# A depthwise convolution in front of an expert layer: normalising by channels, a ring of spread bands, and the next block's front inside the convolution

## What is computed

```python
def _L0_conv_ref(x, w_large, w_small, ...):      # depthwise: one 13x13 and one 3x3 kernel for each channel
    large = bn(dwconv(x, w_large, 6), g_l, b_l, m_l, v_l)
    small = bn(dwconv(x, w_small, 1), g_s, b_s, m_s, v_s)
    return large + small + bn(x, g_i, b_i, m_i, v_i)
...
x = x + _L0_conv_ref(_ln_c(x), ...)              # _ln_c: mean and variance over the 96 channels of a pixel
t = _to_tokens(x)
t = t + _L0_ffn_ref(_ln_t(t), ...)               # 4 experts 96 -> 384 -> 96, the two best by a softmax gate
```

## Time and profile before

| | |
|---|---|
| median of 3 runs | 1277.17 us (1275.31 to 1277.45) |
| the profiled execution: time, and span of its profile | 1275.62 us, 1273.5 us |
| busy over the span: PE, PEld, DVE, ACT, POOL | 92%, 80%, 63%, 38%, 20% |
| mean granted TensorE clock | 0.957 of full speed |
| TensorE's first instruction; first convolution matmul; end of the last one; first `moe_up` matmul | 25.4, 30.1, 86.5, 98.6 us |

### The profile page before, as it was taken

One profiled execution on the slowest core, in us unless ns is written; L12 is line 12 of the kernel. 1 busy time (PEld: TensorE's weight loads), 2 busy tenths in 40 slices (PEclk: granted clock), 3 DMA queues, 4 the chain that ended last, 5 costly groups with the idle time before them and its releaser, 6 DMA issues. The chain is left out here.

```text
span 1273.5 us, 24179 instructions
## 1 busy us (share of the span) xinstructions
PE 1171.1 (92%) x8528; PEld 1024.4 (80%) x8528; DVE 807.9 (63%) x2916; ACT 482.4 (38%) x944; POOL 254.0 (20%) x234
## 2 busy tenths in 40 slices
PE   1979999947999999999999999999999998999776
PEld 1978999946999999899997767767999987887555
DVE  6036676646666665587775565655777767776646
ACT  3514334323555544334431323223334322332442
POOL 3002112122010100312122333332221222211200
PEclk9998999977999999899999999999999999999786
DMA  3301000010000000000000000000000000000000
GB/s 136 86 4 66 20 31 19 1 50 1 2 2 1 2 1 1 2 1 0 0 1 1 2 1 2 2 1 2 1 1 0 0 1 1 1 1 4 1 11 37
DMA packets 11562, 15.69 MB, mean 12 GB/s; under 512 B 7385, under 2 KB 9007, under 8 KB 11346
## 3 DMA queue, kind: packets, MB, share of 16 engines
q1 hardware_dynamic: 10754, 12.86, 3.1%
q10 hardware_dynamic: 720, 1.66, 0.3%
HBM read 11.37 MB, written 3.15 MB: 11 GB/s over the span
## 5 line engine op out<-in xcount | busy, mean ns | idle before, releaser
L955 PEld LDWEIGHTS moe_dn<-all_w,moe_hid 128*128 128x128 f32 x2304 | 269.9, 192 | 5.4
L955 PE MATMUL moe_dn<-all_w,moe_hid 128*128 128x96 f32 x2304 | 271.7, 275 | 0.0
L890 ACT ACTIVATE moe_hid<-moe_up 128x512 f32<-128x512 f32 x288 | 169.7, 598 | 231.2 <-PE moe_up L947 218.1
L945 PE MATMUL moe_up<-front_xh,front_w1h 97*128 97x512 f32 x288 | 121.9, 423 | 0.6 <-PEq L1005 0.3
L835 DVE SCALAR_TENSOR_TENSOR all_X<-moe_dn,front_gate,all_X 128x96 f32 (+1 forms) x384 | 95.3, 310 | 30.5 <-PE moe_dn L955 24.4
L947 PE MATMUL moe_up<-front_xl,front_w1h 97*128 97x512 f32 x288 | 113.8, 395 | 0.0
L946 PE MATMUL moe_up<-front_xh,front_w1l 97*128 97x512 f32 x288 | 113.3, 393 | 0.0
L827 DVE SCALAR_TENSOR_TENSOR all_X<-all_b,front_gate,all_X 128x96 f32 (+1 forms) x384 | 100.8, 324 | 6.2 <-DVE front_var L81 2.8
L786 POOL TENSOR_TENSOR front_prob<-front_euler,front_logit 128x16 f32<-128x16 f32 x21 | 60.9, 2901 | 189.9 <-DVEq L414 189.9
L1386 PE MATMUL l1c_o<-l1c_vs,l1c_pt 128*128 128x64 f32 x768 | 94.4, 277 | 0.5 <-DVE l1c_ro L1164 0.5
L1386 PEld LDWEIGHTS l1c_o<-l1c_vs,l1c_pt 128*128 128x128 f32 x768 | 91.8, 195 | 2.9 <-issue 0.9
(11 more groups left out here) (401 smaller groups left out, 2019.5 us busy)
## 6 DMA issues: line engine op xcount, KB each, us to landing
all_w<-w SPq DMA_DIRECT2D x3, 582.0 KB
all_w<-w SPq DMA_DIRECT2D x3, 576.0 KB
all_X<-x_rows SPq DMA_DIRECT2D x2, 768.0 KB, 6.8
conv_scratch<-all_X SPq DMA_DIRECT2D x2, 768.0 KB, 3.2
all_X<-conv_scratch SPq DMA_DIRECT2D x2, 768.0 KB, 4.7
out_tokens<-l3f_y SPq DMA_DIRECT2D x5, 288.0 KB, 2.1
l0c_band<-band ACTq DMA_DIRECT2D x1, 1248.0 KB, 9.3
all_b<-b SPq DMA_DIRECT2D x3, 192.0 KB
```

The source lines that it names most:

```text
L890: act.activation(hid[:, n, :], up[n % UPS][:, :], ACT.Gelu).then_inc(hid_done, 1)
L945: pe.matmul(bank, w1h[:, n, :], xh[:, p, :], start=True, stop=False)
L955: last = pe.matmul(dn[e % 2][:, j * C:(j + 1) * C], hid[:, n, j * P:(j + 1) * P], w2[:, n, :], start=(k == 0), stop=(k == KC - 1))
```

## The change

In `l0_conv`:
- The tokens are normalised by channels in three chunks (channels 0 to 15, 16 to 47, 48 to 95). For each chunk and half of the images there are two instructions, a subtraction that reads `X` with the tile as the inner dimension, and a product in place. Turn 0 needs chunk 0 alone; turns 1 to 5 are moved behind convolution pieces 0, 1, 2, 4 and 6.
- POOL's power for the batch norms is cut in two: 9 values for groups 0 to 2 first, then the tokens' two powers, then 27 values.
- `full` is a ring of six groups, filled group by group, three groups ahead.
- Groups 10 and 11 are done by halves of the images, first half first: pieces (10, half 0), (11, half 0), (10, half 1), (11, half 1), so 14 pieces in all.
- The expert layer's front is moved into this block: its weights are split behind pieces 4 to 9, its constants are set early, and its statistics, normalising and transposes follow the adding back of piece 11, which completes the first half of the images. The first convolution's `dve_binarise` is cut in two around it.

In `moe`, layer 0 keeps of the front only the gate's matmuls, logits, softmax and choice; the choice comes behind the statistics of step 1.

```diff
@@ WeightWork
-    def dve_binarise(self, dve, chain):
+    def dve_differences(self, dve, chain):
         dve.wait_ge(self.signs, 1)
         dve.tensor_tensor(sg[0:C, 0, :], sg[0:C, 0, :], w1[0:C, :], ALU.subtract)
         chain.sync(dve.tensor_tensor(sg[:, 1, 0:KC * C], sg[:, 1, 0:KC * C], w2f, ALU.subtract))
+    def dve_binarise(self, dve, chain):
         dve.tensor_tensor(w1[0:C, :], w1[0:C, :], sg[0:C, 0, :], ALU.add)
         dve.tensor_tensor(w2f, w2f, sg[:, 1, 0:KC * C], ALU.add)
@@ l0_conv
+        RF, FIRST = 6, 3
+        CHUNKS = (0, 2 * GC, 6 * GC, C)
-        full = s.sb("full", [P, NG * KL, GC, SIDE])
+        full = s.sb("full", [P, RF, KL, GC, SIDE])
+        F = T["front"].begin(s, T, 0, front_tp, None)
+        SPLIT = NG - 2
+        PIECES = [(g, 0, 2) for g in range(SPLIT)] + [(g, h, h + 1) for h in range(2) for g in range(SPLIT, NG)]
+        TURN_AFTER = {0: 1, 1: 2, 2: 3, 4: 4, 6: 5}
@@ gpsimd
-            pool.tensor_tensor(inv[:, :, :], shift[:, :, :], mhalf[:, :].rearrange("p (k g) -> p k g", k=3),
-                               ALU.pow).then_inc(bn_pow, 1)
+            factors(0, FIRST)
...
+            factors(FIRST, NG)
+            F.pool_consts(pool)
+            F.pool_rstd(pool)
@@ scalar
+            def fill(g):
+                act.wait_ge(band_done, 1 if g < FIRST else 2)
+                if g >= RF:
+                    act.wait_ge(conv_done, g - RF + 1)
                 for k in range(GC):
+                    last = act.activation(full[:, g % RF, :, k, :], band[:, g, :, :], ACT.Copy, scale=own[:, k:k + 1])
...
+            fill(0)
+            tokens_out(0)
+            fill(1)
+            fill(2)
+            for n in range(NP):
+                if n in TURN_AFTER:
+                    tokens_out(TURN_AFTER[n])
+                conv_copy(n)
+                if n + 3 < NG:
+                    fill(n + 3)
+                if 4 <= n < 4 + NE:
+                    F.act_weights(act, n - 4)
+                if n == 8:
+                    F.act_consts(act)
+                if n == SPLIT + 1:
+                    work.act_signs(act)
+            F.act_tokens(act)
@@ vector
+            def normalise(c):
+                lo, hi = CHUNKS[c], CHUNKS[c + 1]
+                for h, half in enumerate(halves):
...
+                    out = xn[:, h, lo:hi, :]
+                    chain.sync(dve.tensor_tensor(out, x0[:, half, lo:hi].rearrange("p t c -> p c t"), wide(mean),
+                                                 ALU.subtract))
+                    last = dve.tensor_tensor(out, out, wide(rstd), ALU.mult)
+                last.then_inc(xn_done, 1)
+            merge_bands(0, 0, FIRST)
+            for c in range(len(CHUNKS) - 1):
+                normalise(c)
+            merge_bands(1, FIRST, NG)
...
+            for n in range(NP):
+                add_back(n)
+                if n == NG - 6:
                     work.dve_sums(dve, chain)
+                if 6 <= n < 6 + NE:
+                    F.dve_weights(dve, n - 6)
+                if n == NG - 3:
                     work.dve_centre(dve, chain)
+                if n == SPLIT + 1:
+                    dve.wait_ge(back_out, n + 1)
+                    F.dve_stats(dve, chain)
+                    work.dve_differences(dve, chain)
+                    F.dve_apply(dve, chain)
+                if n == SPLIT + 2:
+                    work.dve_binarise(dve, chain)
+            F.dve_low(dve)
@@ tensor
+            turn(0)
+            for n in range(NP):
+                conv_piece(n)
+                if n in TURN_AFTER:
+                    turn(TURN_AFTER[n])
+                if n >= 1:
+                    turn_back(n - 1)
+                if n == NG - 3:
                     work.pe_means(pe)
+            F.pe_turn(pe)
+            turn_back(NP - 1)
@@ moe
-                F.dve_stats(dve, chain)
-                F.dve_apply(dve, chain)
-                for e in range(NE):
-                    F.dve_weights(dve, e)
-                    if e == 0:
-                        F.dve_low(dve)
-                F.dve_logits(dve, chain)
-                F.dve_gates(dve, chain)
+                F.dve_logits(dve, first)
...
+                if layer == 0 and isinstance(g, int) and g == 0:
+                    F.dve_gates(dve, first)
-                F.pe_turn(pe)
                 F.pe_gates(pe)
-                pe.wait_ge(F.w_low, 1)
-                pe.wait_ge(F.xl_done, 1)
```

More of the change, by code:

```diff
@@ L278, in _, with tokens_out @@
             act.dma_start(own[:, :], A["own"]).then_inc(w_in, 16)
-            def fill(chunk):
-                groups = slice(chunk * FG, (chunk + 1) * FG)
-                rows = slice(chunk * FG * KL, (chunk + 1) * FG * KL)
+            def fill(g):
+                act.wait_ge(band_done, 1 if g < FIRST else 2)
+                if g >= RF:
+                    act.wait_ge(conv_done, g - RF + 1)
                 for k in range(GC):
-                    last = act.activation(full[:, rows, k, :], band[:, groups, :, :].rearrange("p g r x -> p (g r) x"),
-                                          ACT.Copy, scale=own[:, k:k + 1])
+                    last = act.activation(full[:, g % RF, :, k, :], band[:, g, :, :], ACT.Copy, scale=own[:, k:k + 1])
                 last.then_inc(full_done, 1)
-            act.wait_ge(band_done, 1)
-            fill(0)
-            for g2 in range(NG // 2):
+            def tokens_out(g2):
                 act.wait_ge(turned, g2 + 1)
@@ L319, in _ @@
                 dve.sem_inc(ln_var, 1)
[L320 to L325, removed]
@@ L363, in _, with turn @@
             ident = T["ident"]
-            pe.wait_ge(ident_in, 16)
-            pe.wait_ge(xn_done, 2)
-            for g2 in range(NG // 2):
+            def turn(g2):
+                pe.wait_ge(xn_done, next(c for c in range(len(CHUNKS)) if CHUNKS[c] >= 2 * GC * (g2 + 1)))
                 if g2 >= 2:
@@ L388, in conv_group, with turn_back @@
                 last.then_inc(conv_done, 1)
-            def turn_back(g):
-                pe.wait_ge(conv_out, g + 1)
-                if g >= 2:
-                    pe.wait_ge(back_out, g - 1)
-                for h in range(2):
-                    last = pe.transpose(bp[g % 2][:, h * P:(h + 1) * P], conv[:, g % 2, h * P:(h + 1) * P],
+            def turn_back(n):
+                g, first, end = PIECES[n]
+                pe.wait_ge(conv_out, n + 1)
+                if n >= 2:
+                    pe.wait_ge(back_out, n - 1)
+                for h in range(first, end):
+                    last = pe.transpose(bp[n % 2][:, h * P:(h + 1) * P], conv[:, n % 2, h * P:(h + 1) * P],
@@ L960, in step @@
                 for e in range(1, NE):
-                    if layer == 0 and isinstance(g, int) and g == 0:
-                        wait(pe, F.w_low, e + 1)
                     ups(g, p, e)
```

139 lines of the change are left out of this document (72 added, 67 removed).

## The result

The changed kernel took 1267.9 us in the median of 6 runs (1265.7 to 1271.2), the kernel before 1276.4 (1273.5 to 1277.8) in 6 runs beside it: ratio 0.9935, 95% interval 0.9917 to 0.9954. That is 8.5 us less; 8.7 were predicted. The profiled execution took 1267.7 us (span 1265.7), and the span of the one before was 1273.5: 7.8 us less between these two.

What follows compares the result with a forecast made beforehand. Two TensorE holes (25.4 and 6.9 us of waits) around a TensorE-bound convolution; 9.7 - 1.6 - 2.2 - 2.6 - 0.2 + 5.6 = 8.7 us off 1277.2 gives 1268.5 us, range 1266.0 to 1271.0.

Steps and rivals of the forecast that it cites:

- Start of piece 0: Convolution head: first turn at 18.6 us, piece 0 at 20.4 instead of 30.1, a gain of 9.7 us.
- rival 2: Convolution ring filled late through slow short fills or strided reads, so piece 3 waits: 1270 to 1276 us, chance 0.12.
- factor f: Normalising on DVE: slowdown of the strided subtractions, which take 3.2 us at full rate and end 3.2(f - 1) later.
- the cover of 3.7: Convolution loop: ACT is through at 33.6 us, piece 3 is due at about 37.3, so no stall.
- Rival 3: Normalising: strided read at f of 5 or more makes the kernel slower, 1280.8 us at f = 6; chance 0.03.
- Cold start: Piece 0: TensorE first runs at half clock, a loss of 1.6 us, the middle of 0.65 and 2.55.
- Turns between the pieces: Convolution loop: five turns moved between the pieces cost 5 x 4 x 0.109, 2.2 us.
- Halves: Groups 10 and 11: 2.9 us a half, 11.6 against 9.0, loss 2.6; two pairs of turn-backs cost 0.2.
- Tail: Convolution's end to first expert matmul: 6.5 us after the last piece's matmuls instead of 12.1, a gain of 5.6.
- E: Convolution's end: the time when the last piece's matmuls end, from which the steps to the first expert matmul are counted.
- rival 1: Block switch to the expert layer: TensorE's clock stays up, gain 12.0 us, 1265.2 us; chance 0.22.
- rival 4: Whole kernel: it does nothing, the earlier start being taken back by unseen waits; 1277 us, chance 0.03.

Runs made afterwards that it cites:

- experiment 6: Changed kernel plus 24 matmuls on the identity, results unread, ahead of the first turn: 1263.8 us, ratio 0.9902 to the kernel before.
- the tail alone: Changed kernel with the head as before (all tokens normalised and turned first), a ring of nine groups: ratio 1.0002 to the kernel before; twelve runs spread over 10.6 us.
- experiment 8: Changed kernel with DVE's two sign differences behind the front's normalising; one execution: group 10 to first expert matmul 18.77 us instead of 18.97.
- experiment 11: The changed kernel again, unaltered, on the same chip as its two combined variants: 1269.0 us, ratio 0.9938 to the kernel before.
- the head alone: Changed kernel with groups 10 and 11 whole and the front back in the expert block: 1272.0 us, ratio 0.9962 to the kernel before.
- 5: Changed kernel plus unread identity matmuls, 8 before the front's transposes and 9 behind the last turn-back: 1265.3 us, ratio 0.9917 to the kernel before.
- Kernel 10: Changed kernel plus 24 identity matmuls before the first turn, earlier turn-backs of pieces 11 and 12, seven idle matmuls behind the last turn-back: 1261.8 us, ratio 0.9889.
- kernel 9: Changed kernel plus 24 identity matmuls before the first turn and turn-backs of pieces 11 and 12 behind the successor's fifth tap: 1261.9 us, ratio 0.9887.

## Why the prediction came out right, point by point

**Start of piece 0: 9.7 us predicted, 9.0 measured.** TensorE's first turn came at 19.33, not 18.6. Half of the 0.7 us is DVE's start (17.17 where the sum had 16.8). The other half is the strided subtraction: 0.59 us for 256 elements where the product in place beside it takes 0.42, and 1.05 and 1.50 against 0.69 and 0.96 for 512 and 768. The increments are 1.8 ns an element against 1.04, so rival 2's factor f, taken as 1, is 1.7. `xn` is done at 27.4 us where the sum had 24.9; the cover of 3.7 holds, and TensorE has no wait in the loop. Rival 3 would have needed 4.9. The subtraction differs from the product also in writing to another tile; but the front's subtraction of 512 elements in rows (`front_xl`), which does so too, takes 0.69 us like the product, so it is the step of 96 floats that costs. The Trainium skill (SBUF — State Buffer, section Door 1: The DMA port swizzle) has a penalty for such accesses and no size of it. These rows agree, and the size here is a factor of 1.7.

The powers of POOL had been worked out by a line through 4, 16 and 36 values. In the trace after:

```profile
6.12 1.80 POOL L282 TENSOR_TENSOR l0c_inv<-l0c_shift,l0c_mhalf 128x9 f32<-128x9 f32 x1 [5.28 <-DVEq L348]
...
13.78 2.90 POOL L289 TENSOR_TENSOR l0c_rstd<-l0c_var,l0c_mhalf 128x16 f32<-128x16 f32 x1 [1.20 <-DVEq L354]
16.64 4.64 POOL L282 TENSOR_TENSOR l0c_inv<-l0c_shift,l0c_mhalf 128x27 f32<-128x27 f32 x1
```

1.80 and 4.64 us for 9 and 27 values (1.8 and 4.7 predicted). The fill took 0.37 us an instruction (0.33, bounds 0.24 and 0.45), all under turn 0.

**Cold start: 1.6 predicted, 1.4 measured, but the term is not a fixed one.** The eight executions that start cold with one turn lost 1.4 to 2.9 us against the 5.04 of the warm ones, in the middle 2.3 to 2.5. The bounds were 0.65 and 2.55; the three largest values, 2.71 and twice 2.88, lie above. The profiled execution hit the low end, which was luck, and 1.6 was too small. The value in the middle would have taken 0.8 off the sum. The prediction calls this the clock. The granted clock of the profile does not show it: it reads 1.00 from 0 to 30 us in every kernel that starts cold, while the passes run at half the rate. What is shown is the spacing of the passes, and that work of TensorE ahead of them takes the loss away (experiment 6). That transposes count as nothing for the clock, the rule of the Trainium skill (TensorE: Matmul & The Clock Gate, Part 4: PE-mode transpose), is spoken against a second time, as far as the spacing tells the clock, by the tail alone, whose TensorE did nothing but 24 transposes before its piece 0:

```profile
26.28 4.43 PE L433 MATMUL l0c_tp<-all_ident,l0c_xn 128*128 128x128 f32 x20 [26.28 <-DVE l0c_xn L91]
30.86 0.63 PE L433 MATMUL l0c_tp<-all_ident,l0c_xn 128*128 128x128 f32 x4 [0.16 <-ACT l0c_xt L311]
31.33 5.99 PE L450 MATMUL l0c_cp<-l0c_xt,l0c_full 128*128 128x256 f32 x34
```

The first 20 run 0.22 us apart, the last four 0.11 (0.63 with the tail of the last), and the 34 passes behind them at full rate. With matmuls instead of waiting in front, the transposes are warm from the first:

```profile
11.41 7.47 PE L65 MATMUL l0c_cp<-all_ident 128*128 128x128 f32 x48 [11.41 <-DMA all_ident<-ident]
19.38 0.66 PE L432 MATMUL l0c_tp<-all_ident,l0c_xn 128*128 128x128 f32 x4 [0.50 <-DVE l0c_xn L390]
20.74 4.76 PE L451 MATMUL l0c_cp<-l0c_xt,l0c_full 128*128 128x256 f32 x26 [0.70 <-ACT l0c_xt L312]
```

**Turns between the pieces: 2.2 predicted; a turn took 0.44 us (27.14 to 27.58), five 2.2. Halves: 2.6 predicted.** A half takes 2.97 us with its turn-back of 0.11, so 0.110 a pass; four cost 11.4 against 9.0: 2.4 us. The `moe_dn` row was the right neighbour: the passes of 80 to 128 columns took what one of 96 took there.

**Tail: 5.6 predicted, 5.1 measured.** TensorE's wait was 2.07 us (2.1 predicted). The first expert matmul came at E + 7.0 (E = 83.9), not E + 6.5. The transposes started 0.24 us late (86.25); POOL's power, 1.37 instead of 1.01 us beside DVE's differences, is enough for that, and without it (experiment 8) they start at E + 1.9. The tokens' low part ended at 88.73, 0.3 late in all, and the block's switch took 0.45 us, to 89.2, instead of 0.3. The gates at half the clock took 1.70 to the next, as put down.

Sum of the measured terms: 9.0 - 1.4 - 2.2 - 2.4 - 0.2 + 5.1 = 7.9, against 7.7 at the first expert matmul. So the mechanism of each term came out, and the sizes did not cancel: the head was 0.7 us too good, the tail 0.5, and the cold start and the halves gave back 0.2 each. At the first expert matmul the sum of 8.7 was 1.0 us too high, and it would have been more with a cold piece of the usual length. That the medians came out at 8.5 is in part luck, since the runs of the changed kernel alone spread over 5.5 us. Its repetition on another occasion (experiment 11) has 1269.0 against 1276.9: 7.9.

**What the parts are worth, by undoing them.** At the first expert matmul the head alone gives 4.6 us, the halves 1.8, the front's move without them 0.65 and the rest of the 7.7 is the cold piece, 0.75 us longer in the head's execution.

**Rivals.** The clock fell in spite of the shorter holes (rival 1), in every kernel but those with matmuls put into them (5 and 10). The ring was never late: no kernel has a wait of TensorE for `full` in its first 90 us (rival 2). The gain at the first expert matmul arrived at the end (rival 4).

**What was missed** is not in the sum, but was to be had: 6 to 7 us more, from a few changed lines. The changed kernel leaves TensorE a cold start of 1.4 to 2.9 us, an order of turn-backs that costs 1.8, and a lower clock behind it that costs 2.8. Kernel 10, which removes all three, has its first `moe_dn` at 91.26, 6.1 us before the changed kernel's first profile and 8.3 before its second (97.37 and 99.55). By the medians kernel 9 is 7.1 us under the changed kernel on the same chip (1261.9 against 1269.0) and 15.0 under the one before. But three of its five runs are of the shorter sort, and the two profiled executions, both at 0.55 in their last 21.7 us, are 4.6 us apart in their spans (1264.1 and 1268.7), as they are at the first `moe_dn` (4.7).

## What to carry to other kernels

Where TensorE starts on the first part of its input, ask what is ready before that part: matmuls on a constant in the waiting time take the slow start away, and cost nothing as long as they end before that part is there. Where a late consumer hangs on a short TensorE instruction behind a long series, put that instruction into the series as soon as its input is there; halving a piece helps only as far as its result leaves the queue. And read small gains at a marker close behind the change: the end-to-end times of one kernel spread over 5.5 us (the changed one, six runs) and up to 10.6 (experiment 2). The marker has to lie behind the stretch at the lower clock, whose length varies. At the first expert matmul experiment 6 is 1.5 us ahead of the changed kernel; at the first `moe_dn` it is 0.74, and at TensorE's first instruction of layer 1 0.72 (265.16 against 265.88).

## What the runs showed of the hardware that was not expected

- A DVE subtraction of f32 with a step of 96 floats took 0.59, 1.05 and 1.50 us for 256, 512 and 768 elements, in place with a step of one 0.42, 0.69 and 0.96.
- A cold TensorE's first group of 26 passes took between 6.2 and 7.65 us in two executions of one kernel, from starts 0.04 us apart.
- POOL's power of 4 values took 1.37 us beside two DVE instructions of 384 and 288 elements, 1.01 without.
- The granted clock reads 1.00 over the first 30 us while the first transposes and passes run at half the rate of the later ones (0.20 to 0.22 and 0.11 us a transpose).
- The last three groups of 12 `l3f_dn` passes took 2.88 us each in the changed kernel's profile and 1.58 in that with whole groups, with the same code and the same idle time of 1.99 us before the first of them: the granted clock of the last 21.7 us is 0.55 in seven of the 13 profiles and 0.88 in six.
